# The sum of squares over channels: from a matmul with ones to a turn on VectorE and a DRAM scratch

## The chip, the cores and the metric

The kernel runs on one core of a Trainium2 chip. The time is device time in microseconds (us) from the first to the last instruction of one execution, the median over several. The kernel before takes 1737.63 us, median of 3 runs (1737.61 to 1738.3).

A core has TensorE (PE, matmuls and their weight loads), VectorE (DVE), ScalarE (ACT), GpSimd (POOL) and SyncE (SP), which here only issues DMAs. Each runs its own list of instructions in order; they wait for each other through semaphores. So an instruction that waits holds up all that stands behind it on its engine.

## The reference

Two sequences of 512 tokens with 512 channels go through a Mamba-2 block (128 heads in 8 groups) and a feed-forward block, each on the layer-normalised input with a residual. The part that matters here is the gated RMS norm of the Mamba block, per token and group of 1024 channels:

```
g = y * silu(gate)
gg = g.reshape(b, l, G, GS)                       # G = 8, GS = 1024
var = mean(gg * gg, axis=-1, keepdims=True)
g = (gg * rsqrt(var + EPS)).reshape(b, l, INTER) * norm_w
return g @ out_w.T
```

The kernel multiplies by `out_w` first and scales each token of the product by its `rsqrt` afterwards, when it adds it to the residual. So one number per token and group is wanted, `mean_sq`, with the tokens on the 128 partitions. `g` itself lies the other way round, channels on partitions and tokens along them, so the squares have to be summed across partitions.

## The kernel before, in words

All products are in float32 split in two parts (`_h` and `_l`), three matmuls each (`split_product`). Work goes in 64 steps, `K = 8 g + k`: 8 groups `g`, and in each `k` = 0 to 7, of which 0 to 3 are the four chunks of 128 tokens of the first sequence and 4 to 7 those of the second. The prediction calls `k` = 0 the first step of a group, `k` = 1, 2, 5, 6 second and third steps and `k` = 3, 7 fourth steps.

In a step TensorE does, in the order of `body`: the scores (`inside`, 32 matmuls, L1788), the total of the squares of the step before (`square_total`), the new state (`new_state`, not in fourth steps), a projection tile, turning x for the next step (`turn_x`), `match`, `across` (L1803), more projection tiles of the next sequence and group (L1712 to L1714, 12 matmuls each), and between them the two halves of the output product (`out_half`: L1846, L1829, L1836). Projection tiles go alternately into two PSUM banks, so tile i waits until tile i - 2 has been taken out: a gate tile by ScalarE, a convolution tile (`c0` to `c9`) by ScalarE and then three VectorE passes, the taps (L1385). The tiles of a slot are in `SLOT_TILES`: a first step has g0, g1, c0, c1, g2; a second c2, c3, c4, c5, g3; a third c6 to c9, g4; a fourth g5, g6, g7.

The squares: ScalarE squares g into `y` (8 blocks of channels by 128 tokens), GpSimd adds the 8 blocks to one (`square_sum`, `sum_ready`), TensorE multiplies that block by a column of ones (`square_total`, L1862), VectorE adds EPS (`mean_square`, L1481), GpSimd raises to -1/2 (`inverse_root`, L753), VectorE scales the output product and adds it up (`accumulate`, L1487).

Order is written out by hand on each engine. VectorE in a step: `fade`, `add_skip` (waits for the scores), `add_state`, `mean_square` of the step before, `gated`, and then taps, `scale_x` (L1404), `accumulate`, `scale_across`, the decay products (`scores`, L1415); in a first step also the low parts of the output weights (`ow_low`, L1391), which the output product needs. GpSimd in a fourth step: two masks (L710), a weight's low part (L704), `inverse_root`, two masks, `gT_low` (L738), `weigh_x` (L725), `square_sum`, `xw_low` (L733), which `new_state` of the next step waits for. SyncE: four decay loads of 256 KB, each when TensorE is through a quarter of the scores (`in_done`, L481), then ec loads (L487) and the weights of later tiles (L455).

Of the kernel before, what the change touches and what calls it, by code (L numbers as in the profile page):

```python
# [5 lines left out]
F32 = mybir.dt.float32  # L6
# [26 lines left out]
PIECE = KT * P  # L33

# [90 lines left out]
def build(nc, x_in, wp_in, ow_in, wdt_in, par_in, dt_bias_in, a_log_in,  # L125
# [3 lines left out]
    cols_dram = nc.dram_tensor("cols_scratch", (GROUPS, BATCH, P, UNIT_COLS), F32, kind="Internal").ap()  # L129
    cdec_dram = nc.dram_tensor("cdec_scratch", (BATCH, GROUPS, GH * SC), F32, kind="Internal").ap()  # L130

    with ExitStack() as ctx:
# [17 lines left out]
        sb("align", [P, 112])  # L150
# [110 lines left out]

        def total_of(K):

            return xt[1][:, 0:1] if K == MIDDLE else cbb[:, 2 * P:2 * P + 1]

# [65 lines left out]
        ss_done = sem("ss_done")  # L331
# [121 lines left out]
        def _(sp):  # L453
# [35 lines left out]

            def store_rows(b):  # L490
                cs = slice(b * SC, (b + 1) * SC)
                sp.dma_start(rows_dram[cs].rearrange("c h t -> h c t"),
                             ncumT[:, seq(b)].rearrange("p (c t) -> p c t", c=SC)).then_inc(rows_stored, 16)
# [102 lines left out]
            def last_chunk(k):  # L596
                K = LAST * CHUNKS + k
                if k < CHUNKS - 1:
                    for q in range(QUARTERS):
                        sp.wait_ge(in_done, K * QUARTERS + q + 1)  # L600
                        load_decay(LAST, k + 1, q)
                    sp.wait_ge(z_scaled, n_across(LAST, k + 1))
                    load_ec(LAST, k + 1)
                if k == SC:
                    load_up(WRING - 1)
                for p in LAST_PAIRS[k]:
                    if k == CHUNKS - 1 and p == LAST_PAIRS[k][-1]:
                        sp.wait_ge(g_ready, KEND)
                        sp.dma_start(b2_raw, l2_in[:, 0:HID]).then_inc(lora2_loaded, 16)
                        sp.dma_start(a2_raw, l2_in[:, HID:HID + FFN]).then_inc(lora2_loaded, 16)  # L610
                    load_up(2 * p + WRING)
                    load_up(2 * p + 1 + WRING)
                if k == CHUNKS - 1:
                    sp.wait_ge(in_done, KEND * QUARTERS)
                    for m in range(W2RING):
                        load_w2(m)

            def body(g, last):
                for k in range(CHUNKS):
# [21 lines left out]
                    if more:  # L641
                        for q in range(QUARTERS):
                            sp.wait_ge(in_done, K * QUARTERS + q + 1)
                            load_decay(gn, kn, q)
                    if more and kn % SC > 0:
                        if some(n_across(gn, kn)):
                            sp.wait_ge(z_scaled, n_across(gn, kn))
                        load_ec(gn, kn)
# [13 lines left out]
                    if last and k == SC - 1:  # L662
                        first_up()

# [226 lines left out]
        def _(act):  # L891
# [82 lines left out]
            def square(g, k):  # L974
                K, b, c = g * CHUNKS + k, k // SC, k % SC
                act.wait_ge(g_ready, K + 1)
                if some(K):
                    act.wait_ge(ss_done, K)
# [282 lines left out]
            act.wait_ge(ss_done, KEND)  # L1261
# [18 lines left out]
        def _(dve):  # L1280
# [283 lines left out]
            def last_chunk(k):  # L1564
                pairs = LAST_PAIRS[k]
                if k == SC:
# [12 lines left out]
                    return  # L1579
                gate_up(pairs[0] - 1)  # L1580
                fade(LAST, k)
                add_skip(LAST, k)
                add_state(LAST, k)
                mean_square(LAST, k - 1)
                gated(LAST, k)
# [7 lines left out]
                norm_apply(1, k - 1)  # L1593
                if k < CHUNKS - 1:
# [15 lines left out]
            def body(g, last):  # L1610
                for k in range(CHUNKS):
# [16 lines left out]
                    if late:  # L1628
                        norm_apply(1, 0)
                        norm_apply(1, 1)  # L1630
                    if k != 1:
                        fade(g, k)
# [5 lines left out]
                    else:  # L1638
                        add_state(g, k)
                        mean_square(*before)  # L1640
                        gated(g, k)
                    if late:
# [5 lines left out]
                        norm_apply(1, 2)  # L1648
                        for q in range(QUARTERS):
                            scores(gn, kn, q)  # L1650
# [58 lines left out]
        def _(pe):  # L1709
# [55 lines left out]
            def match(g, k):  # L1765
# [3 lines left out]
                if some(K - 1):  # L1769
                    pe.wait_ge(mean_ready, K - 1)  # L1770
# [37 lines left out]
            def new_state(g, k):  # L1808
# [8 lines left out]
                if K == MIDDLE + 1:  # L1817
                    pe.wait_ge(mean_ready, K)
# [141 lines left out]
            def last_chunk(k):  # L1960
                t = 2 * LAST_PAIRS[k][0]
                inside(LAST, k)
                if k > SC:
                    square_total(LAST, k - 1)
# [31 lines left out]
                else:  # L1996
# [7 lines left out]
                    square_total(LAST, k)  # L2004
# [4 lines left out]
            def body(g, last):  # L2009
                for k in range(CHUNKS):  # L2010
# [18 lines left out]
                    if not first:  # L2029
                        square_total(*((g, k - 1) if k else (g - 1, CHUNKS - 1)))  # L2030
# [15 lines left out]
                    if c == SC - 1:  # L2046
# [3 lines left out]
                        if last:  # L2050
                            norm_transpose(1, 2)
                            square_total(g, k)
# [21 lines left out]
            pe.wait_ge(mean_ready, KEND)  # L2074
# [111 lines left out]
```

## Time and profile before

| | |
|---|---|
| median of 3 runs | 1737.63 us |
| span of the profiled execution | 1737.2 us |
| TensorE, matmuls | 1724.5 us busy, 99% |
| TensorE, weight loads (beside matmuls) | 1436.9 us, 83% |
| VectorE | 1221.0 us, 70% |
| ScalarE | 1192.8 us, 69% |
| GpSimd | 1182.1 us, 68% |
| DMA queue of SyncE | 41.7% of 16 engines' span |
| mean granted TensorE clock | 0.999 |

Busy shares are means over the span. Within a step each engine has its own times of full work and of waiting. A timeline row gives the start in us from the span's start, the length, the engine and line, what is written and read, the number of instructions merged into the row, and in brackets the idle time before it. The length of merged rows is from the first start to the last end. The end of a matmul is modelled, and neighbours overlap, so differences between starts tell what a matmul costs.

### The profile page before, as it was taken

The page shows a single profiled execution, that of the slowest core. Times are in us where ns is not written, and L with a number is a line of the kernel's source. Part 1 is how long each engine was busy: PE and PEld are TensorE (multiplying, and loading weights), DVE is VectorE, ACT ScalarE, POOL GpSimd, SP SyncE. Part 2 cuts the span into 40 slices and gives each one's busy share as a digit, 9 for nine tenths or more (in the row PEclk, how much of TensorE's full clock was granted, in tenths as well). Part 3 has the DMA queues.
Part 4 walks back from the last instruction along what each step waited for, and adds up shares of the span by engine and source line. Part 5 has one row for each costly group of instructions (what it writes and reads, how often), then busy time and mean ns, then how long its engine had stood idle before and what let it go on. Part 6 is the DMA issues. An engine that isn't in the chain of part 4 may idle for free.

```text
span 1737.2 us, 27735 instructions
## 1 busy us (share of the span) xinstructions
PE 1724.5 (99%) x9925; PEld 1436.9 (83%) x9925; DVE 1221.0 (70%) x2154; ACT 1192.8 (69%) x2232; POOL 1182.1 (68%) x1058
## 2 busy tenths in 40 slices
PE   9999999999999999999999999999999999999999
PEld 7788888888888888888888888888888888787887
DVE  8886778768785769676875878586867688663323
ACT  6887677767867677767776777768777777663421
POOL 5586768677777668676867687766867686774510
PEclk9999999999999999999999999999999999999999
DMA  5534435343543443443534354345343353444201
GB/s 192 171 107 116 125 116 169 109 119 105 162 128 114 121 146 112 121 116 112 174 115 115 97 162 128 114 122 151 114 118 113 110 174 101 118 114 134 80 15 49
DMA packets 122056, 211.63 MB, mean 122 GB/s; under 512 B 24256, under 2 KB 28992, under 8 KB 121920
## 3 DMA queue, kind: packets, MB, share of 16 engines
q1 hardware_dynamic: 121920, 209.87, 41.7%
q8 instruction: 80, 1.31, 0.3%
q14 instruction: 56, 0.46, 0.1%
HBM read 205.09 MB, written 4.72 MB: 121 GB/s over the span
## 4 chain that ended last, share of the span: by engine, by line
PE 97%; DVE 1%; DMA 1%; POOL 0%; ACT 0%; issue 0%; POOLq 0%
PE bank L1712 19%; PE bank L1714 18%; PE bank L1713 18%; PE bank L1788 7%; PE bank L1846 7%; PE bank L1836 7%; PE bank L1829 7%; PE bank L1803 5%; PE bank L1762 2%; PE bank L2091 1%; PE bank L2092 1%; PE bank L2093 1%; PE bank L1862 1%; PE bank L1772 1%; PE bank L1953 1%; DMA w_raw<-in_wp 0%
## 5 line engine op out<-in xcount | busy, mean ns | idle before, releaser
L704 POOL TENSOR_TENSOR w_l<-w_raw,w_h 128x512 fp32r<-128x512 f32 x288 | 379.6, 1321 | 341.2 <-ACT w_h L900 341.2
L1712 PE MATMUL bank<-x_h,w_h 128*128 128x512 f32 (+1 forms) x1328 | 527.0, 397 | 3.9 <-DVE x_ch L1385 2.3
L1714 PE MATMUL bank<-x_h,w_l 128*128 128x512 f32 (+1 forms) x1328 | 519.7, 391 | 0.0
L1713 PE MATMUL bank<-x_l,w_h 128*128 128x512 f32 (+1 forms) x1328 | 518.1, 390 | 0.0
L1385 DVE SCALAR_TENSOR_TENSOR x_ch<-bank,par,x_ch 128x511 f32<-128x511 f32 (+2 forms) x384 | 287.2, 749 | 80.3 <-ACT x_ch L918 71.2
L953 ACT ACTIVATE decay<-decay,cols 128x128 f32<-128x128 f32 x1024 | 318.2, 390 | 3.7 <-DMA cdec<-cdec_scratch 1.6
L1712 PEld LDWEIGHTS bank<-x_h,w_h 128*128 128x128 f32 (+1 forms) x1328 | 249.5, 188 | 55.1 <-issue 3.1
L1714 PEld LDWEIGHTS bank<-x_h,w_l 128*128 128x128 f32 (+1 forms) x1328 | 249.2, 188 | 54.6
L1713 PEld LDWEIGHTS bank<-x_l,w_h 128*128 128x128 f32 (+1 forms) x1328 | 249.7, 188 | 51.1
L1415 DVE TENSOR_TENSOR decay<-decay,bank 128x512 f32<-128x512 f32 x256 | 171.3, 683 | 107.1 <-ACT decay L953 107.1
L918 ACT ACTIVATE x_ch<-bank,par 128x512 f32<-128x512 f32 x128 | 99.0, 774 | 185.6 <-PE bank L1714 185.5
L710 POOL TENSOR_SCALAR_AFFINE_SELECT decay<-decay 128x512 f32<-128x512 f32 x256 | 173.9, 697 | 65.8 <-DMA decay<-cum_scratch 64.3
L1436 DVE SCALAR_TENSOR_TENSOR bank<-x_ch,par,bank 128x128 f32<-128x128 f32 x512 | 138.4, 350 | 92.8 <-PE bank L1788 92.8
L900 ACT ACTIVATE w_h<-w_raw 128x512 fp32r<-128x512 f32 x288 | 178.7, 621 | 4.4 <-DMA w_raw<-in_wp 4.4
L738 POOL TENSOR_TENSOR gT_l<-sgT,gT_h 128x1024 fp32r<-128x1024 f32 x64 | 153.9, 2405 | 8.2 <-ACT gT_h L972 8.2
L939 ACT ACTIVATE sgT<-bank 128x512 f32<-128x512 f32 x122 | 71.9, 590 | 111.9 <-PE bank L1714 111.7
L1846 PE MATMUL bank<-ow_h,gT_h 128*128 128x512 f32 x512 | 137.3, 390 | 0.0
L1836 PE MATMUL bank<-ow_h,gT_l 128*128 128x512 f32 x512 | 136.9, 389 | 0.0
L1829 PE MATMUL bank<-ow_l,gT_h 128*128 128x512 f32 x512 | 136.9, 389 | 0.0
L1788 PEld LDWEIGHTS bank<-decay,xdt 128*64 128x64 f32 x2048 | 110.5, 137 | 22.6 <-issue 22.6
L1788 PE MATMUL bank<-decay,xdt 128*64 128x128 f32 x2048 | 125.9, 276 | 0.0
L733 POOL TENSOR_TENSOR xw_l<-xw,xw_h 128x1024 fp32r<-128x1024 f32 x48 | 114.9, 2394 | 0.3 <-ACT xw_h L965 0.3
(161 smaller groups left out, 2760.0 us busy)
## 6 DMA issues: line engine op xcount, KB each, us to landing
w_raw<-in_wp SPq DMA_DIRECT2D x288, 256.0 KB, 3.0
decay<-cum_scratch SPq DMA_DIRECT2D x256, 256.0 KB, 4.1
ec<-ecum_scratch SPq DMA_DIRECT2D x96, 256.0 KB, 6.2
ow_raw<-in_ow SPq DMA_DIRECT2D x64, 256.0 KB, 4.8
w_raw<-in_w SPq DMA_DIRECT2D x48, 256.0 KB, 2.7
acc<-in_x SPq DMA_DIRECT2D x8, 256.0 KB, 4.5
out<-acc SPq DMA_DIRECT2D x8, 256.0 KB, 2.0
cols<-cols_scratch SPq DMA_DIRECT2D x16, 96.0 KB, 2.7
```

The costliest lines, as they stand in the source:

```text
L704: pool.tensor_tensor(w_l[:, s, :], w_raw[:, s, :], w_h[:, s, :].bitcast(F32), ALU.subtract).then_inc(wl_ready, 1)
L710: pool.affine_select(out=d, in_=d, compare_op=ALU.is_ge, fill=fill, base=0, pattern=[[0, QH], [1, P]], channel_multiplier=-1).then_inc(mas ...
L900: act.activation(w_h[:, s, :], w_raw[:, s, :], ACT.Copy).then_inc(wh_ready, 1)
L953: last = act.activation(decay[:, h, :], decay[:, h, :], ACT.Exp, bias=cols[:, b, CUM, c, h:h + 1], scale=-1.0)
L1385: dve.scalar_tensor_tensor(out=conv(bu, t)[:, s:], in0=bank_of(u, i)[:, 0:SEQ - s], scalar=w, in1=conv(bu, t)[:, s:], op0=ALU.mult, op1=AL ...
L1712: pe.matmul(dst, wh, xh, start=(opens and k == 0), stop=False)
L1713: pe.matmul(dst, wh, xl, start=False, stop=False)
L1714: last = pe.matmul(dst, wl, xh, start=False, stop=(k == len(terms) - 1 and not more))
L1788: last = pe.matmul(yb[n // 4][a * HDIM:(a + 1) * HDIM, tok(n % 4)], xdt[:, h * HDIM:(h + 1) * HDIM], decay[:, h, :], start=(c == 0), stop= ...
L1829: last = pe.matmul(ob[:, :], gT_h[:, n, :], ow_l[:, n, :], start=False, stop=(k == 0 and n == CT - 1))
L1836: last = pe.matmul(ob[:, :], gT_l[:, n, :], ow_h[:, n, :], start=False, stop=(k > 0 and n == CT - 1))
L1846: pe.matmul(ob[:, :], gT_h[:, n, :], ow_h[:, n, :], start=(n == 0), stop=False)
```

## The change

`square_total` and its 64 matmuls go. In their place VectorE turns the summed block in squares of 32 by 32 (`turn_squares`) and adds up each 32 columns: partition 32 c + t then holds, in column b, the sum over the 32 channels of block c for token 32 b + t. SyncE stores that to a scratch in DRAM (`total_squares`), waits for the landing, and fetches it in four DMAs, one per 32 tokens, so that the four partial sums of a token come to lie side by side. VectorE adds those four and EPS. `mean_square` now stands behind `gated`. `match`, `new_state` and `accumulate`'s neighbours no longer wait for the old bank of the total. The line numbers of the changed kernel are 4 higher on SyncE, and 24 or more higher on VectorE.

```diff
+SQ = 32
+QUADS = P // SQ
...
+    sq_dram = nc.dram_tensor("sq_scratch", (2, P, QUADS), F32, kind="Internal").ap()
...
+            def total_squares(g, k):
+
+                K = g * CHUNKS + k
+                sp.wait_ge(sq_summed, K + 1)
+                sp.dma_start(sq_dram[K % 2], sq_part[:, :]).then_inc(sq_stored, 16)
+                sp.wait_ge(sq_stored, 16 * (K + 1))
+                if some(K):
+                    sp.wait_ge(mean_ready, K)
+                src = sq_dram[K % 2].rearrange("(c t) b -> b t c", c=QUADS)
+                for q in range(QUADS):
+                    sp.dma_start(sq_full[q * SQ:(q + 1) * SQ, :], src[q], allow_slow_non_contiguous=True).then_inc(sq_fetched, 16)
...
                         for q in range(QUARTERS):
                             sp.wait_ge(in_done, K * QUARTERS + q + 1)
                             load_decay(gn, kn, q)
+                            if q == 2 and some(K):
+                                total_squares(*((g, k - 1) if k else (g - 1, CHUNKS - 1)))
...
                     if last and k == SC - 1:
                         first_up()
+                        total_squares(g, k)
...
             def mean_square(g, k):
                 K = g * CHUNKS + k
-                dve.wait_ge(ss_done, K + 1)
-                dve.tensor_scalar(mean_sq[:, :], total_of(K), EPS, None, ALU.add).then_inc(mean_ready, 1)
+                dve.wait_ge(sq_fetched, 16 * QUADS * (K + 1))
+                dve.tensor_reduce(mean_sq[:, :], sq_full[:, :], mybir.AxisListType.X, ALU.add).then_inc(mean_step, 1)
+                dve.wait_ge(mean_step, K + 1)
+                dve.tensor_scalar(mean_sq[:, :], mean_sq[:, :], EPS, None, ALU.add).then_inc(mean_ready, 1)
+
+            def turn_squares(g, k):
+
+                K = g * CHUNKS + k
+                dve.wait_ge(sum_ready, K + 1)
+                dve.transpose(y[:, 1, :], y[:, 0, :]).then_inc(sq_turned, 1)
+                dve.wait_ge(sq_turned, K + 1)
+                if some(K):
+                    dve.wait_ge(sq_stored, 16 * K)
+                dve.tensor_reduce(sq_part[:, :], y[:, 1, :].rearrange("p (b t) -> p b t", b=QUADS),
+                                  mybir.AxisListType.X, ALU.add).then_inc(sq_summed, 1)
...
+                    if not first:
+                        turn_squares(*before)
                     if k != 1:
                         fade(g, k)
                     add_skip(g, k)
...
                         add_state(g, k)
+                        gated(g, k)
                         mean_square(*before)
-                        gated(g, k)
...
-                if some(K - 1):
-                    pe.wait_ge(mean_ready, K - 1)
...
-            def square_total(g, k):
-
-                K = g * CHUNKS + k
-                pe.wait_ge(sum_ready, K + 1)
-                if K == MIDDLE:
-                    pe.wait_ge(xdt_ready, K + 2)
-                pe.matmul(total_of(K), y[:, 0, :], ones[:, :], start=True, stop=True).then_inc(ss_done, 1)
...
-                    if not first:
-                        square_total(*((g, k - 1) if k else (g - 1, CHUNKS - 1)))
```

SyncE's list in the first step of a group, from the last output weight ahead of the decay loads on; `sq_part` and `sq_full` are the two small SBUF tiles, 128 by 4. Before:

```order
L469 DMA ow_raw<-in_ow 128x512
L481 DMA decay<-cum_scratch 128x512 [waits in_done] x4
L487 DMA ec<-ecum_scratch 64x1024 [waits z_scaled]
L487 DMA ec<-ecum_scratch 64x1024
L455 DMA w_raw<-in_wp 128x512 [waits pj_done]
```

and now:

```order
L473 DMA ow_raw<-in_ow 128x512
L485 DMA decay<-cum_scratch 128x512 [waits in_done] x3
L498 DMA sq_scratch<-sq_part 128x4 [waits sq_summed]
L504 DMA sq_full<-sq_scratch 32x4x1 [waits mean_ready,sq_stored]
L504 DMA sq_full<-sq_scratch 32x4x1 x3
L485 DMA decay<-cum_scratch 128x512 [waits in_done]
L491 DMA ec<-ecum_scratch 64x1024 [waits z_scaled]
L491 DMA ec<-ecum_scratch 64x1024
```

The fourth decay load, and all behind it, now stand behind a store, a wait for its landing and four fetches.

VectorE's list in such a first step, from `add_state` on; `ow_l` are the output weights' low parts. Before:

```order
L1475 COPY state<-bank 128x512 [waits st_done]
L1475 COPY state<-bank 128x512
L1481 TENSOR_SCALAR mean_sq<-bank 128x1 [waits ss_done]
L1449 TENSOR_TENSOR sgT<-bank,sgT 128x4x128 [waits y_ready,gate_done]
L1449 TENSOR_TENSOR sgT<-bank,sgT 128x4x128
L1391 SCALAR_TENSOR_TENSOR ow_l<-ow_raw,par,ow_h 128x512 [waits owh_ready] x2
L1404 TENSOR_TENSOR xdt<-bank,cols 128x512 [waits xw_ready,in_done,tx_done]
L1404 TENSOR_TENSOR xdt<-bank,cols 128x512
L1487 SCALAR_TENSOR_TENSOR acc<-bank,rstd,acc 128x512 [waits rstd_ready,out_done]
L1391 SCALAR_TENSOR_TENSOR ow_l<-ow_raw,par,ow_h 128x512 [waits owh_ready] x4
```

and now:

```order
L1499 COPY state<-bank 128x512 [waits st_done]
L1499 COPY state<-bank 128x512
L1473 TENSOR_TENSOR sgT<-bank,sgT 128x4x128 [waits y_ready,gate_done]
L1473 TENSOR_TENSOR sgT<-bank,sgT 128x4x128
L1505 TENSOR_REDUCE mean_sq<-sq_full 128x1 [waits sq_fetched]
L1507 TENSOR_SCALAR mean_sq<-mean_sq 128x1 [waits mean_step]
L1415 SCALAR_TENSOR_TENSOR ow_l<-ow_raw,par,ow_h 128x512 [waits owh_ready] x2
L1428 TENSOR_TENSOR xdt<-bank,cols 128x512 [waits xw_ready,in_done,tx_done]
L1428 TENSOR_TENSOR xdt<-bank,cols 128x512
L1524 SCALAR_TENSOR_TENSOR acc<-bank,rstd,acc 128x512 [waits rstd_ready,out_done]
L1415 SCALAR_TENSOR_TENSOR ow_l<-ow_raw,par,ow_h 128x512 [waits owh_ready] x4
```

The mean has moved behind `gated` (L1473) and waits for the fetches instead of the matmul; all the `ow_l`, `xdt` and `acc` work stands behind it.

## Rows read from the trace of the kernel before

**Rows 1.** The page, chain that ended last: share of the span by engine.

```profile
PE 97%; DVE 1%; DMA 1%; POOL 0%; ACT 0%; issue 0%; POOLq 0%
```

**Rows 2.** Groups of TensorE by line: busy us, mean ns of one, idle before.

```profile
L1862 PE MATMUL bank<-ones,y 128*128 128x1 f32 x128 | 24.4, 260 | 0.3 <-POOL y L748 0.3
```

**Rows 3.** Timeline (start us, length us), TensorE, step without a total.

```profile
82.67 1.97 PE L1788 MATMUL bank<-decay,xdt 128*64 128x128 f32 x32
...
84.90 0.40 PE L1713 MATMUL bank<-x_l,w_h 128*128 128x512 f32 x1
```

**Rows 4.** Timeline, TensorE: a fourth step and the next one.

```profile
717.12 1.97 PE L1788 MATMUL bank<-decay,xdt 128*64 128x128 f32 x32
...
734.14 1.97 PE L1788 MATMUL bank<-decay,xdt 128*64 128x128 f32 x32
...
736.28 0.48 PE L1712 MATMUL bank<-xw_h,b_tok_h 128*128 128x512 f32 x1
736.59 0.40 PE L1713 MATMUL bank<-xw_l,b_tok_h 128*128 128x512 f32 x1
```

**Rows 5.** Timeline, SyncE's queue, in the fourth step at 717.12.

```profile
717.81 1.75 SPq L481 DMA_DIRECT2D decay<-cum_scratch  x4
```

**Rows 6.** Its third decay load alone, issued at 718.7.

```profile
DMA to landing us min/median/max: 4.3/4.3/4.3
```

**Rows 7.** DMA issues: count, KB each, us from issue to landing.

```profile
out<-acc SPq DMA_DIRECT2D x8, 256.0 KB, 2.0
...
a_log<-in_a_log SPq DMA_DIRECT2D x1, 0.5 KB, 4.2
```

**Rows 8.** The second store of cdecT (2 KB), landing alone.

```profile
DMA to landing us min/median/max: 1.7/1.7/1.7
```

**Rows 9.** Groups of VectorE by line.

```profile
L1412 DVE TENSOR_TENSOR b_tok_l<-bank,b_tok_h 128x128 fp32r<-128x128 f32 x64 | 18.0, 281 | 0.0
...
L1481 DVE TENSOR_SCALAR mean_sq<-bank 128x1 f32<-128x1 f32 x64 | 9.7, 151 | 1.2 <-PE bank L1862 1.2
```

**Rows 10.** Timeline, GpSimd, fourth step at 717.12.

```profile
724.77 0.55 POOL L753 TENSOR_TENSOR rstd<-mean_sq,minus_half 128x1 f32<-128x1 f32 x1
...
733.31 2.38 POOL L733 TENSOR_TENSOR xw_l<-xw,xw_h 128x1024 fp32r<-128x1024 f32 x1
```

**Rows 11.** Timeline, TensorE, first step of a group.

```profile
640.30 1.97 PE L1788 MATMUL bank<-decay,xdt 128*64 128x128 f32 x32
...
656.74 1.07 PE L1829 MATMUL bank<-ow_l,gT_h 128*128 128x512 f32 x4
...
660.37 0.39 PE L1712 MATMUL bank<-x_h,w_h 128*128 128x512 f32 x1
```

**Rows 12.** Timeline, SyncE's queue, the same step.

```profile
642.78 2.17 SPq L481 DMA_DIRECT2D decay<-cum_scratch  x4
```

**Rows 13.** Its third decay load alone, issued at 643.7.

```profile
DMA to landing us min/median/max: 6.2/6.2/6.2
```

**Rows 14.** Timeline, VectorE, the same step.

```profile
646.58 1.41 DVE L1391 SCALAR_TENSOR_TENSOR ow_l<-ow_raw,par,ow_h 128x512 fp32r<-128x512 f32 x2
...
649.94 0.75 DVE L1487 SCALAR_TENSOR_TENSOR acc<-bank,rstd,acc 128x512 f32<-128x512 f32 x1 [0.76 <-POOL rstd L753]
650.61 5.26 DVE L1391 SCALAR_TENSOR_TENSOR ow_l<-ow_raw,par,ow_h 128x512 fp32r<-128x512 f32 x4
...
657.37 2.31 DVE L1385 SCALAR_TENSOR_TENSOR bcT<-bank,par,bcT 128x511 f32<-128x511 f32 x3
```

**Rows 15.** Timeline, TensorE, a second step.

```profile
759.74 1.97 PE L1788 MATMUL bank<-decay,xdt 128*64 128x128 f32 x32
...
771.66 0.39 PE L1712 MATMUL bank<-x_h,w_h 128*128 128x512 f32 x1
```

**Rows 16.** Timeline, VectorE, the same second step.

```profile
767.12 2.32 DVE L1385 SCALAR_TENSOR_TENSOR x_ch<-bank,par,x_ch 128x511 f32<-128x511 f32 x3 [1.01 <-ACT x_ch L918]
```

More of the change, by code:

```diff
@@ L149, in build @@
         mean_sq, rstd = sb("mean_sq", [P, 1]), sb("rstd", [P, 1])
-        sb("align", [P, 112])
+        sq_part, sq_full = sb("sq_part", [P, QUADS]), sb("sq_full", [P, QUADS])
+        sb("align", [P, 104])
         scan_ctx = ExitStack()
@@ L260, in build @@
         MIDDLE = (GROUPS - 1) * CHUNKS + SC - 1
-        def total_of(K):
-            return xt[1][:, 0:1] if K == MIDDLE else cbb[:, 2 * P:2 * P + 1]
         def normed(k, c, squares, gates):
@@ L330, in build @@
         out_done = sem("out_done")
-        ss_done = sem("ss_done")
+        sq_turned = sem("sq_turned")
+        sq_summed = sem("sq_summed")
+        sq_stored = sem("sq_stored")
+        sq_fetched = sem("sq_fetched")
+        mean_step = sem("mean_step")
         decay_seen = sem("decay_seen")
@@ L597, in last_chunk @@
                 K = LAST * CHUNKS + k
+                if k == CHUNKS - 1:
+                    total_squares(LAST, k - 1)
                 if k < CHUNKS - 1:
@@ L601, in last_chunk @@
                         load_decay(LAST, k + 1, q)
+                        if q == 2 and k > SC:
+                            total_squares(LAST, k - 1)
                     sp.wait_ge(z_scaled, n_across(LAST, k + 1))
@@ L614, in last_chunk @@
                     sp.wait_ge(in_done, KEND * QUARTERS)
+                    total_squares(LAST, k)
                     for m in range(W2RING):
@@ L977, in square @@
                 if some(K):
-                    act.wait_ge(ss_done, K)
+                    act.wait_ge(sq_summed, K)
                 act.activation(y[:, :, :], sgT[:, b, :, tok(c)], ACT.Square, scale=GCH ** -0.5).then_inc(sq_ready, 1)
@@ L1260, in _ @@
             act.wait_ge(out_done, 2 * KEND)
-            act.wait_ge(ss_done, KEND)
+            act.wait_ge(sq_summed, KEND)
             for m in range(FT):
@@ L1579, in last_chunk @@
                     return
+                turn_squares(LAST, k - 1)
                 gate_up(pairs[0] - 1)
@@ L1583, in last_chunk @@
                 add_state(LAST, k)
+                gated(LAST, k)
                 mean_square(LAST, k - 1)
-                gated(LAST, k)
                 if k < CHUNKS - 1:
@@ L1593, in last_chunk @@
                 norm_apply(1, k - 1)
+                if k == CHUNKS - 1:
+                    turn_squares(LAST, k)
                 if k < CHUNKS - 1:
@@ L1648, in body @@
                         norm_apply(1, 2)
+                        turn_squares(g, k)
                         for q in range(QUARTERS):
@@ L1816, in new_state @@
                     pe.wait_ge(x_l_ready, CHUNKS + k - 1)
-                if K == MIDDLE + 1:
-                    pe.wait_ge(mean_ready, K)
                 for h in range(2):
@@ L1962, in last_chunk @@
                 inside(LAST, k)
-                if k > SC:
-                    square_total(LAST, k - 1)
                 new_state(LAST, k)
@@ L2003, in last_chunk @@
                     out_half(LAST, k, 1)
-                    square_total(LAST, k)
                     up(t + 4)
@@ L2051, in body @@
                             norm_transpose(1, 2)
-                            square_total(g, k)
                         out_half(g, k, 1)
@@ L2073, in _ @@
             pe.wait_ge(lora2_l_ready, 2)
-            pe.wait_ge(mean_ready, KEND)
             pe.wait_ge(acc_ready, KEND)
```

## The prediction

> **What bounds the kernel now.** I read the page first, then the groups by line, then timelines of three kinds of step. The chain that ended last is TensorE for 97% of the span [rows 1], so the time is TensorE's own work plus whatever makes it wait; nothing off TensorE shortens it. The removed total is in 128 matmul records (two for each of 64 totals), 24.4 us busy in sum, with 0.3 us of waiting in the whole run [rows 2]. Work beside TensorE is free until it makes one of TensorE's waits come true, so what matters is how much room each wait has. I call a step's start T, the moment its first L1788 matmul starts; there are 64 steps, eight to a group.
>
> **What is removed.** Matmuls overlap, so 24.4 us is not what goes. In step 0, which has no total, the second product behind the scores starts 84.90 - 82.67 = 2.23 us after T [rows 3]; with a total in between it is 736.59 - 734.14 = 2.45 us [rows 4]. So one total costs 0.22 us, 64 of them 14.1 us. The upper end is 24.4 us, the lower 0. The wait of `match` for `mean_ready` also goes; it ended no idle time of TensorE worth a row, so nothing is late in its place and I take 0.
>
> **What is added, and on which path.** The mean square of a step is now made in the next one: VectorE turns and sums (`turn_squares`), SyncE stores 2 KB, waits for the landing, issues four fetches, and VectorE finishes in `mean_square`, behind which its own queue stands still. SyncE does this between the third and the fourth decay load.
>
> *When the mean is there, ordinary step.* The four decay loads start at 717.81 and take 1.75 us to issue, 0.44 each [rows 5], so the third is out at T + 2.0 and the store goes at T + 2.0. That third load lands 4.3 us after its issue at 718.7, at T + 5.9 [rows 6]. The store has the same queue and the same DMA engines as the three loads of 256 KB ahead of it. Bounds for its landing: 1.7 us after issue, as a 2 KB store did with little else in flight [rows 8], which is T + 3.7, and 4.2 us, as a 0.5 KB load did behind other transfers [rows 7], T + 6.2. I take T + 6.0, just behind the load ahead, since that is the nearest row in the same place. Four fetches at 0.44 us start from T + 6.1, the last at T + 7.4. Each has 128 pieces of 4 bytes; its landing lies between 1.7 [rows 8] and 4.2 us [rows 7]. I take 2.0, the row of the stores at the end, which also go through an empty queue [rows 7]: T + 9.4. The reduction and the addition are 0.15 us each by the tiny operation they replace [rows 9], 0.1 for the semaphore between them: the mean is ready at T + 9.8. SyncE itself comes 5.8 us later (T + 7.8 instead of 2.0) to the fourth decay load, the ec loads and the next weights. Behind them GpSimd's fourth mask and ScalarE's w_h wait; by the timelines the mask has its turn just behind the later rstd anyway and the weights are needed four tiles ahead, so I count 0 there and keep up to 1 us per step for the range.
>
> The Trainium skill weighs in twice here, from "DMA: Bandwidth & Descriptors". Its section "Anatomy of one DMA" gives a DMA a fixed 2.0 us and very little for size: the store would then land at T + 4.0 whatever is ahead of it, which is the first rival below. Its section "Queues, rings and completion order" says that an engine takes a queue's descriptors in ring order and that the completion write lands only behind earlier writes: that gives T + 6.0, my value. No run so far shows a 2 KB store behind decay loads.
>
> *Fourth steps* (positions 3 and 7 of groups 0 to 6: 14). GpSimd starts rstd at 724.77 and then runs without a gap through masks, gT_l, xw, the square sum and xw_l, which ends at 735.69: 10.92 us [rows 10]. TensorE needs xw_l at 736.28, 0.59 us later [rows 4]. After: rstd starts at T + 9.85, xw_l ends at T + 20.8. TensorE gets there at 17.02 + 1.90 = T + 18.9 (next T, then 32 score matmuls and no total). It waits 1.9 us, in all 14 x 1.9 = 26 us.
>
> *First step of a group* (7, groups 1 to 7). SyncE starts its decay loads only at 642.78 [rows 12], behind parameter, weight and ow loads. The third lands 6.2 us after 643.7, at T + 9.6 [rows 13]. The same sum gives store landed 9.7, last fetch issued 11.1, down at 13.1, mean at T + 13.5. VectorE stood at T + 6.3 before where its ow_l starts [rows 14] and its queue is nearly full: two ow_l (1.41) to 14.9, xdt (1.2) to 16.2, acc (0.7) to 16.9, four ow_l (5.26, so 2.6 for two) to 19.5 and 22.1, state fade (1.5) to 23.6, the taps of tile c0 (2.3) to 25.9 [rows 14]. TensorE wants the fourth ow_l at 656.74, T + 16.4, and c0's bank for tile g2 at 660.37, T + 20.1 [rows 11]; both come 0.2 earlier without the total. It waits 19.5 - 16.2 = 3.3, and then 25.9 - (19.9 + 3.3) = 2.7 us: 6.0 a group, 42 us.
>
> *Second and third steps* (positions 1, 2, 5, 6; 30 in all, 23 without those right behind a first step). VectorE's taps of the slot's first tile stand behind `mean_square`: they start at 767.12 now and take 2.32 [rows 16]; after, T + 9.8 + 2.3 = 12.1. TensorE writes over that bank at 771.66, T + 11.9 [rows 15], 11.7 without the total: 0.4 us, 23 x 0.4 = 10 us.
>
> *The rest.* `turn_squares` is two operations over 128 columns, 0.3 us each by the row of that size [rows 9], before add_skip, where VectorE idles for PE in most steps; it costs where VectorE is late, in the step behind a first one. With step 3 of group 7, where the store stands behind the first FFN weights, I put 8 us for all this, 3 to 15 for the range. Moving `gated` ahead of the mean is what keeps g_half in time; it gains 0.1 us at most.
>
> Sum: 26 + 42 + 10 + 8 = 86 us of waits, less 14 us. The profiled execution spans 1737.2 us and the median of the runs is 1737.6, 0.4 more. So 1737.6 + 72, about 1809 us.
>
> **Rivals.**
> *Short landings.* The store lands 2.0 us after its issue, not behind the loads. Ordinary steps have the mean at T + 7.8, xw_l ends at 18.8 against 18.9: no wait. In a first step the third load is issued at T + 3.9, so the store is down at 5.9, the mean at 9.7: taps end at 22.1 against 19.9, 2.2 us, 7 x 2.2 = 15. With 4 for the rest: 1737.6 + 19 - 14 = 1743 us. For it: landings of 1.7 and 2.0 us exist [rows 7, 8]; against: both have nothing big ahead.
> *Slow small pieces.* Each fetch takes the 4.2 us of the 4-byte-piece load [rows 7], so the mean is 2.2 us later: fourth steps 4.1 x 14 = 57, first steps 8.2 x 7 = 57, second and third 2.6 x 23 = 60, rest 10; 184 - 14 gives 1908 us. For it: the only row with such pieces. Against: that load stood behind others of 256 KB at the start.
> *All hidden, faster.* Only the 0.22 us per total counts: 1737.6 - 14 = 1723.5 us. The point that decides is the mean in a first step: the taps there end 12.4 us behind it, so at T + 7.5 or sooner TensorE waits for nothing. But even the third decay load lands at T + 9.6 there. It would need the store to overtake and VectorE to have slack that its timeline doesn't show.
>
> **How the numbers follow.** Forecast 0.65, short landings 0.16, slow pieces 0.14, hidden 0.05. Within the forecast, a landing 0.5 us sooner or later moves the mean by as much in 44 steps, 22 us, and the rest by 7: 1780 to 1840. For 8 in 10 I reach towards both rivals: 1752 to 1880. A change within 0.2% (3.5 us) can't be told from none here. Hidden is faster; of short landings a fifth or so may come out same or faster. Faster 0.06, same 0.03, slower 0.91.
>
> **What would show it.** Right: TensorE has new waits, for xw_l in the step behind a fourth one (about 1.9 us), for ow_l and for x_ch or bcT taps in a first step (3.3 and 2.7); VectorE's idle time before the reduction of sq_full is 3 to 5 us in ordinary steps and about 7 in first ones, ended by the DMA; the store of sq_part lands about 4 us after issue in ordinary steps, 5.5 in first ones; fetches land 2 us after issue. Wrong: if the store lands in 2 us (short landings), if the fetches need 4 (slow pieces), if masks wait for the fourth decay load and so add a price that I put at 0, or if TensorE waits in all steps alike.

## The result, and the profile after

The changed kernel takes 1856.24 us, median of 4 runs (1853.38 to 1859.18), against 1737.97 us (1737.61 to 1738.37) for the kernel before beside it: 118 us more, ratio 1.0677, 95% interval 1.0662 to 1.0692. The profiled execution spans 1855.5 us at a mean granted clock of 0.988. The forecast was 1809, its range 1752 to 1880: the sign and part of the mechanism held, and the forecast was 47 us short.

The page after: busy time by engine, and the chain that ended last, by engine and by line (answers to [rows 1]).

```profile
PE 1767.1 (95%) x9797; PEld 1432.5 (77%) x9797; DVE 1246.6 (67%) x2346; ACT 1195.8 (64%) x2232; POOL 1188.3 (64%) x1058
...
PE 62%; DMA 17%; DVE 10%; SPq 5%; issue 3%; POOL 3%; ACT 1%; POOLq 0%; DVEq 0%
PE bank L1755 11%; PE bank L1757 11%; PE bank L1756 11%; DMA sq_scratch<-sq_part 9%; PE bank L1829 6%; PE bank L1875 6%; PE bank L1885 5%; PE bank L1868 5%; DMA decay<-cum_scratch 3%; SPq L504 3%; DMA sq_full<-sq_scratch 3%; DVE ow_l L1415 2%; PE bank L1844 2%; DVE x_ch L1409 2%; POOL gT_l L762 2%
```

TensorE was 97% of the chain and is 62%. The landing of the small store alone is 9% of the span, more than 150 us of the chain for 64 stores of 2 KB. TensorE is idle for 1855.5 - 1767.1 = 88.4 us, before 1737.2 - 1724.5 = 12.7: 75.7 us of new waits. Who ends them stands in the list of TensorE's waits after (total us, times, longest). "issue" means that the profile shows no releaser; the x_ch wait of 2.4 us stands in the kernel before too, with 2.3:

```profile
PE bank L1875 <- POOL gT_l L762: 22.9, 14, 2.1
PE bank L1755 <- DVE x_ch L1409: 14.2, 18, 2.4
PE bank L1755 <- DVE bcT L1409: 13.8, 7, 2.0
PE bank L1755 <- issue: 10.3, 11, 1.0
PE bank L1885 <- issue: 5.3, 7, 1.2
PE bank L1755 <- POOL xw_l L757: 3.5, 1, 3.5
```

The largest, for `gT_l`, is none that the prediction had. The groups of three of the new instructions on VectorE, and of two on ScalarE and GpSimd that wait longer for DMAs than before, where it was 4.4 us for w_h and 65.8 for decay (busy us, mean ns of one, idle before and its releaser):

```profile
L1505 DVE TENSOR_REDUCE mean_sq<-sq_full 128x1 f32<-128x4 f32 x64 | 10.1, 157 | 224.0 <-DMA sq_full<-sq_scratch 224.0
L1513 DVE STREAM_TRANSPOSE y<-y 128x128 f32<-128x128 f32 x64 | 19.5, 304 | 5.6 <-POOL y L772 5.6
L1517 DVE TENSOR_REDUCE sq_part<-y 128x4 f32<-128x128 f32 x64 | 18.3, 286 | 2.2
...
L924 ACT ACTIVATE w_h<-w_raw 128x512 fp32r<-128x512 f32 x288 | 179.3, 623 | 87.5 <-DMA w_raw<-in_wp 87.5
L734 POOL TENSOR_SCALAR_AFFINE_SELECT decay<-decay 128x512 f32<-128x512 f32 x256 | 175.3, 698 | 92.4 <-DMA decay<-cum_scratch 91.6
```

VectorE stands idle for 224 us, 3.5 a step, in front of the mean. Issues to landing (count, KB each, median us), which answer to [rows 7, 8]:

```profile
sq_full<-sq_scratch SPq DMA_DIRECT2D x256, 0.5 KB, 1.8
...
sq_scratch<-sq_part SPq DMA_DIRECT2D x64, 2.0 KB, 3.6
```

*A fourth step and the head of the next.* The timelines after, first of SyncE's queue, then of GpSimd, then of TensorE; T, the start of the first score matmul, is 860.28. They answer to [rows 4, 5, 10].

```profile
860.98 1.28 SPq L485 DMA_DIRECT2D decay<-cum_scratch  x3
862.30 0.43 SPq L498 DMA_DIRECT2D sq_scratch<-sq_part  x1
865.84 1.74 SPq L504 DMA_DIRECT2D sq_full<-sq_scratch  x4
867.62 0.43 SPq L485 DMA_DIRECT2D decay<-cum_scratch  x1
```

```profile
869.41 0.56 POOL L777 TENSOR_TENSOR rstd<-mean_sq,minus_half 128x1 f32<-128x1 f32 x1 [1.64 <-DVE mean_sq L1507]
869.93 0.65 POOL L734 TENSOR_SCALAR_AFFINE_SELECT decay<-decay 128x512 f32<-128x512 f32 x1
872.07 0.64 POOL L734 TENSOR_SCALAR_AFFINE_SELECT decay<-decay 128x512 f32<-128x512 f32 x1 [1.50 <-DMA decay<-cum_scratch]
872.67 2.37 POOL L762 TENSOR_TENSOR gT_l<-sgT,gT_h 128x1024 fp32r<-128x1024 f32 x1
...
879.46 2.37 POOL L757 TENSOR_TENSOR xw_l<-xw,xw_h 128x1024 fp32r<-128x1024 f32 x1
```

```profile
872.60 1.07 PE L1868 MATMUL bank<-ow_l,gT_h 128*128 128x512 f32 x4
875.09 1.19 PE L1875 MATMUL bank<-ow_h,gT_l 128*128 128x512 f32 x4 [1.42 <-POOL gT_l L762]
876.12 1.08 PE L1885 MATMUL bank<-ow_h,gT_h 128*128 128x512 f32 x4
877.04 1.07 PE L1868 MATMUL bank<-ow_l,gT_h 128*128 128x512 f32 x4
...
881.93 0.47 PE L1755 MATMUL bank<-xw_h,b_tok_h 128*128 128x512 f32 x1 [1.02 <-issue]
```

The reader is to see one thing after another: the store goes at T + 2.0 and is down at T + 5.5, the fetches go, and only then, at T + 7.3 instead of T + 2.0, the fourth decay load. It lands at T + 11.6. GpSimd has done rstd and the third mask by T + 10.3, stands 1.50 us for that load, and `gT_l`, next on its list, is 1.42 us late for TensorE. `xw_l` ends at 881.83 and TensorE starts 0.1 later, another 1.02 us lost. The profile names no releaser for that wait, but in all ten such rows TensorE starts 0.1 us behind the end of `xw_l`.

*The first step of a group.* The chain that ended last, in order of time (start, length, what), in the step at 878.94; it answers to [rows 11 to 14].

```profile
882.38 5.45 DMA sq_scratch<-sq_part
887.84 0.32 SPq L504
...
890.41 1.78 DMA sq_full<-sq_scratch
...
892.22 0.17 DVE mean_sq L1505
...
892.48 1.21 DVE ow_l L1415 x2
...
895.09 0.66 DVE acc L1524
895.75 4.05 DVE ow_l L1415 x4
899.80 1.57 DVE state L1482
901.37 0.67 DVE bcT L1409
...
903.74 0.47 PE bank L1755
```

It is the chain that the prediction wrote down for the second wait of such a step, link by link: store, fetch, mean, ow_l, acc, ow_l, state, taps, and TensorE waiting for the bank.

### The profile page after: what moved, and what is told of

Same layout as the page of the kernel before. It is cut to its first block, busy times and chain, and to the rows that moved or that the text cites. A ratio compares the mean times of both kernels' runs of the same rounds, so it can differ in the third digit from the quotient of the medians.

```text
span 1855.5 us, 28055 instructions
## 1 busy us (share of the span) xinstructions
PE 1767.1 (95%) x9797; PEld 1432.5 (77%) x9797; DVE 1246.6 (67%) x2346; ACT 1195.8 (64%) x2232; POOL 1188.3 (64%) x1058
## 4 chain that ended last, share of the span: by engine, by line
PE 62%; DMA 17%; DVE 10%; SPq 5%; issue 3%; POOL 3%; ACT 1%; POOLq 0%; DVEq 0%
PE bank L1755 11%; PE bank L1757 11%; PE bank L1756 11%; DMA sq_scratch<-sq_part 9%; PE bank L1829 6%; PE bank L1875 6%; PE bank L1885 5%; PE bank L1868 5%; DMA decay<-cum_scratch 3%; SPq L504 3%; DMA sq_full<-sq_scratch 3%; DVE ow_l L1415 2%; PE bank L1844 2%; DVE x_ch L1409 2%; POOL gT_l L762 2%
## 5 line engine op out<-in xcount | busy, mean ns | idle before, releaser
L1755 PE MATMUL bank<-x_h,w_h 128*128 128x512 f32 (+1 forms) x1328 | 539.4, 406 | 30.6 <-DVE x_ch L1409 14.2
L1757 PE MATMUL bank<-x_h,w_l 128*128 128x512 f32 (+1 forms) x1328 | 528.9, 398 | 0.0
L1756 PE MATMUL bank<-x_l,w_h 128*128 128x512 f32 (+1 forms) x1328 | 528.8, 398 | 0.0
L1409 DVE SCALAR_TENSOR_TENSOR x_ch<-bank,par,x_ch 128x511 f32<-128x511 f32 (+2 forms) x384 | 286.6, 747 | 10.8 <-ACT x_ch L942 1.6
L924 ACT ACTIVATE w_h<-w_raw 128x512 fp32r<-128x512 f32 x288 | 179.3, 623 | 87.5 <-DMA w_raw<-in_wp 87.5
L1875 PE MATMUL bank<-ow_h,gT_l 128*128 128x512 f32 x512 | 140.5, 397 | 22.9 <-POOL gT_l L762 22.9
L1505 DVE TENSOR_REDUCE mean_sq<-sq_full 128x1 f32<-128x4 f32 x64 | 10.1, 157 | 224.0 <-DMA sq_full<-sq_scratch 224.0
L1885 PE MATMUL bank<-ow_h,gT_h 128*128 128x512 f32 x512 | 144.0, 404 | 8.1 <-issue 5.3
L1460 DVE SCALAR_TENSOR_TENSOR bank<-x_ch,par,bank 128x128 f32<-128x128 f32 x512 | 138.1, 349 | 18.4 <-PE bank L1829 18.2
L1868 PE MATMUL bank<-ow_l,gT_h 128*128 128x512 f32 x512 | 141.6, 399 | 0.0
L1875 PEld LDWEIGHTS bank<-ow_h,gT_l 128*128 128x128 f32 x512 | 96.3, 190 | 48.9 <-POOL gT_l L762 29.0
```

The source lines that it names most:

```text
L924: act.activation(w_h[:, s, :], w_raw[:, s, :], ACT.Copy).then_inc(wh_ready, 1)
L1409: dve.scalar_tensor_tensor(out=conv(bu, t)[:, s:], in0=bank_of(u, i)[:, 0:SEQ - s], scalar=w, in1=conv(bu, t)[:, s:], op0=ALU.mult, op1=AL ...
L1755: pe.matmul(dst, wh, xh, start=(opens and k == 0), stop=False)
L1756: pe.matmul(dst, wh, xl, start=False, stop=False)
L1757: last = pe.matmul(dst, wl, xh, start=False, stop=(k == len(terms) - 1 and not more))
L1868: last = pe.matmul(ob[:, :], gT_h[:, n, :], ow_l[:, n, :], start=False, stop=(k == 0 and n == CT - 1))
```

## The experiments

Two theories stood at first. **A**: VectorE and all behind it wait for the mean. **B**: SyncE's queue, standing still for the store, brings the fourth decay load and later loads late, whoever needs the mean. A third, **C**, came later, from a number that neither explained.

**The DMAs kept, but nobody waits for the fetches.** (This kernel and the two without DMAs leave out the sum across partitions.)

```diff
-                dve.wait_ge(sq_fetched, 16 * QUADS * (K + 1))
-                dve.tensor_reduce(mean_sq[:, :], sq_full[:, :], ...
+                dve.wait_ge(sq_summed, K + 1)
+                dve.tensor_reduce(mean_sq[:, :], sq_part[:, :], ...
```

> Store, wait and fetches of the changed kernel stay on SyncE, but VectorE's mean reads the partial sums of its own partition and waits for no fetch (the sum over partitions is left out). Theory A, that the late mean in VectorE's queue costs most: the 118 us fall to about 20 (1745 us), and fourth steps are back near 17 us. Theory B, that SyncE's blocked queue costs most (the fourth decay load goes out at T + 7.3 instead of 2.0, so GpSimd's fourth mask and gT_l behind it come late): fourth steps stay at 18.7 us or more, and only the first steps get short; 1770 us or more.

1811.61 us, ratio 1.0413 [1.0397, 1.0428]. Only 45 of the 118 us hang on the wait for the mean. TensorE still waits 28.9 us for `gT_l`, 15 times, and fourth steps still take 18.4 to 23.0 us, against 17.0 before. First steps fall back to 26 to 27 us from 29 to 32: there it is the mean. So A alone is refuted, and over half of the loss must lie elsewhere.

**No DMAs at all.** As the last one, and `total_squares` returns at once.

> As the changed kernel, with the turn and sums on VectorE, but no store and no fetch; the mean reads the partial sums of its own partition (the sum over partitions is left out). Both theories: all waits go, and what is left is 0.22 us less per total: 1737.6 - 14 = 1724 us, at most 3 more for the turn. If the turn itself is dear, 1730 or more.

1747.69 us, ratio 1.0050 [1.0031, 1.0069]. So SyncE's waits and the traffic cost 1811.6 - 1747.7 = 64 us. TensorE was idle for 59.9 us in the last kernel and is for 13.2 in this one; 38 us of the difference are its waits for `gT_l` and `xw_l`, as B says. But 1724 was expected, and this has no new waits of TensorE worth a row. With the total gone its steps should be 0.22 us shorter. Most take 25.75 us instead of 25.61, and fourth steps 16.95 instead of 17.02. Something of the change costs over 20 us and is neither A nor B.

**Where SyncE stops: behind the fourth decay load, or ahead of all four.**

```diff
-                            if q == 2 and some(K):
+                            if q == 3 and some(K):
```

> The changed kernel with store, wait and fetches behind the fourth decay load instead of ahead of it. Theory A: the mean comes 0.5 to 1 us later, so 10 to 25 us slower than the changed kernel (1866 to 1880). Theory B: the fourth mask is no longer late, so fourth steps lose about 1 us each and the whole is faster, 1835 to 1845. Both at once: near 1856.

1863.57 us, ratio 1.0711 [1.0695, 1.0727]. Fourth steps fall (17.7 to 18.5 us in most groups) and no wait for `gT_l` is left in the list. But VectorE's wait for the mean grows from 224.0 to 270.6 us, 0.7 a step, and TensorE waits 28.5 us for the x_ch taps where it waited 14.2. What one place gains the other gives back. The time lies between the two ranges, 2 us below A's, and fourth steps moved as B says.

> The changed kernel with store, wait and fetches ahead of all four decay loads. The store has nothing big ahead of it in ordinary steps and should land in 1.7 to 2 us, the mean is ready at about T + 6, and all decay loads go out 3.3 us later. Theory A: about 1770. Theory B: the masks of fourth steps come 1 to 3 us late, 1790 or more.

With `total_squares` ahead of the four loads: 1819.03 us, ratio 1.0458 [1.0440, 1.0475]. First steps take 27.2 to 28.1 us instead of 29 to 32, while `gT_l` still costs 8.7 us in 18 waits. That lies in B's range (1790 or more), but the shorter first steps are A's: both theories carry part of the time. The store of this kernel, with no load ahead of it in its own step, lands 1.4 us after its issue (median); behind three loads it took 3.6:

```profile
sq_scratch<-sq_part SPq DMA_DIRECT2D x64, 2.0 KB, 1.4
```

**The total twice, in the kernel before**, to measure its price.

> The kernel before, with each total's matmul made twice. If a total costs TensorE 0.22 us, as the starts behind it say, 64 more cost 14 us: 1752. If it costs its share of the chain (0.31 us), 20 us: 1758. If it hides, nothing.

1751.54 us against 1737.95, ratio 1.0072 [1.0058, 1.0086]: 13.6 / 64 = 0.21 us each. The gain of the change was sized right.

**Turn, store and fetches early**, in the step that makes the squares, so that nothing waits for a landing.

```diff
-                            if q == 2 and some(K):
-                                total_squares(*((g, k - 1) if k else (g - 1, CHUNKS - 1)))
...
-                        total_squares(g, k)
+                    total_squares(g, k)
...
-                    if not first:
-                        turn_squares(*before)
...
+                    if c < SC - 1:
+                        turn_squares(g, k)
                     taps_of(tiles[3:-1])
...
+                    if c == SC - 1:
+                        turn_squares(g, k)
```

> The changed kernel with the turn put in the step of the squares itself (behind the third decay product, in fourth steps at the end) and store, wait and fetches at the end of SyncE's list of that step, behind its last weight load. In three of four steps the mean has then landed about when the next step starts, in fourth steps at T + 6 of the next, and decay loads are late only there, by 3 us. Theory A and B both: 1724 to 1732, faster than both kernels. If the fetches at a step's start collide with something else, 1740 or more.

1780.27 us, ratio 1.0238 [1.0223, 1.0253]. The forecast missed by 50 us, although second steps of the second half of a group (k = 5) have no wait. Again the steps without a wait are longer than they should be, 25.7 us where 25.4 were due.

```diff
-        sb("align", [P, 104])
+        sb("align", [P, 96])
```

> The kernel before, with nothing of the change, whose filler is 8 elements longer, so every tensor behind it starts 32 bytes further, as in the changed kernel. Placement theory: 24 us slower than before, 1762 us, steps of 25.9 us, the projection's three matmuls 0.70 us. Rival: 1738 us, unchanged.

> The kernel without the DMAs (VectorE takes the mean from its own partial sums, so the sum over partitions is left out), as before, with one thing changed: the filler tensor is 8 elements shorter, so every tensor behind it starts at the byte it has in the kernel before instead of 32 bytes further. Placement theory: the projection's three matmuls are back at 0.68 us from 0.70, 1328 such triples at 6 ns a matmul give 24 us, so 1724 us and steps of 25.4 us. Rival (the slower matmuls come from the order of the instructions, the turn's traffic or the missing total): 1747 us, unchanged.

> The changed kernel with the filler 8 elements shorter, every later tensor at its old address. Placement theory: 24 us less than 1856, so 1832 us, within 8 us of it, with the waits of TensorE unchanged in sum (76 us). Rival: 1856, unchanged; or more than 10 us above 1832 if a faster projection only leaves TensorE waiting longer for the same transfers.

> The kernel with turn, store and fetches in the step of the squares (1780 us), with the filler shorter as well. Placement theory: 24 us less, 1756 us; still above the kernel before by about 18 us, which its own waits make. Rival: 1780, unchanged.

| kernel | shifted by 32 bytes | at the old bytes | difference |
|---|---|---|---|
| before | 1760.08 (ratio 1.0131 [1.0116, 1.0147]) | 1737.58 | 22.5 |
| change without DMAs | 1747.69 | 1729.20 (0.9948 [0.9935, 0.9960]) | 18.5 |
| change | 1856.24 | 1841.10 (1.0593 [1.0579, 1.0608]) | 15.1 |
| early | 1780.27 | 1761.65 (1.0141 [1.0127, 1.0155]) | 18.6 |

C is shown, in both directions and without anything else of the change. A gain of 24 us was forecast for each of the three kernels put back to the old bytes, and they gained 15 to 19: TensorE's busy time fell by 18 to 23 us, but its idle time grew by 2.0, 5.3 and 3.2 us. Without the DMAs and at the old bytes the steps are back at 25.37 and 16.78 us, 0.24 shorter than before the change, as the missing total wants it. TensorE's groups by line, of the kernel before and of the same kernel shifted (mean ns behind the comma):

```profile
L1712 PE MATMUL bank<-x_h,w_h 128*128 128x512 f32 x1312 | 520.6, 397 | 3.9 <-DVE x_ch L1385 2.3 <-POOL w_l L704 1.5
L1714 PE MATMUL bank<-x_h,w_l 128*128 128x512 f32 x1312 | 513.4, 391 | 0.0
...
L1846 PE MATMUL bank<-ow_h,gT_h 128*128 128x512 f32 x512 | 137.3, 390 | 0.0
L1836 PE MATMUL bank<-ow_h,gT_l 128*128 128x512 f32 x512 | 136.9, 389 | 0.0
```

```profile
L1712 PE MATMUL bank<-x_h,w_h 128*128 128x512 f32 x1312 | 526.1, 401 | 3.1 <-DVE x_ch L1385 2.2 <-POOL w_l L704 0.9
L1714 PE MATMUL bank<-x_h,w_l 128*128 128x512 f32 x1312 | 518.7, 395 | 0.0
...
L1846 PE MATMUL bank<-ow_h,gT_h 128*128 128x512 f32 x512 | 139.0, 393 | 0.0
...
L1836 PE MATMUL bank<-ow_h,gT_l 128*128 128x512 f32 x512 | 136.9, 389 | 0.0
```

Each of 3936 projection matmuls is 4 to 5 ns slower, 11 us in these two groups and 6.6 more in the third, L1713: 17.4 of the 21.7 us by which TensorE is busier. Of their operands only the weights are shifted. In the output product both operands are shifted, and there L1836 is not slower at all and L1846 1.7 us in sum. Why the one product suffers and the other hardly does was not told apart, nor were shifts other than 32 bytes tried. In the early kernel the other 32 us above 1729 are new waits for 22.5 us (37.7 us of idle TensorE against 15.2), small ones by many releasers, the largest `bcT` taps with 5.1 us in 9 waits. VectorE now turns and adds in front of them; that this is the cause no run shows.

**B by itself**: the changed kernel at the old bytes, with the store where it was and SyncE's wait and the four fetches behind the fourth decay load.

```diff
                             if q == 2 and some(K):
                                 total_squares(...)
+                            if q == 3 and some(K):
+                                fetch_squares(...)
```

> The changed kernel at its old addresses (1841 us), with SyncE's wait for the store and the four fetches moved behind the fourth decay load; the store keeps its place behind the third. Queue theory (what costs the fourth steps is that SyncE waits with the fourth decay load behind the store, so that GpSimd's last mask and gT_l come late): the fourth load is issued near T+3 instead of T+7.5, the 25 us that TensorE waits for gT_l go, fourth steps fall from a mean of 19.6 us to 18.3, 14 of them and the step behind each give 25 to 30 us: 1811 to 1816 us. Rival (the fetches now stand behind the fourth load's packets and land later, which all steps pay): the mean comes near T+11 and the time stays at 1841 us or above.

1822.32 us, ratio 1.0477 [1.0463, 1.0492], 19 us less than 1841. SyncE's queue and GpSimd in one of its fourth steps, T = 750.6:

```profile
752.66 0.43 SPq L498 DMA_DIRECT2D sq_scratch<-sq_part  x1
753.13 0.43 SPq L485 DMA_DIRECT2D decay<-cum_scratch  x1
756.18 1.74 SPq L507 DMA_DIRECT2D sq_full<-sq_scratch  x4
```

```profile
760.24 1.23 POOL L744 TENSOR_SCALAR_AFFINE_SELECT decay<-decay 128x512 f32<-128x512 f32 x2
761.43 2.42 POOL L772 TENSOR_TENSOR gT_l<-sgT,gT_h 128x1024 fp32r<-128x1024 f32 x1
```

The fourth load goes at T + 2.5, the masks run without a gap, `gT_l` starts 10.8 us after T instead of 12.4, and of TensorE's 25.4 us for it 0.2 are left. Fourth steps fall from 19.7 to 17.9 us, below the 18.3 expected. In this step the mean is not later (T + 9.0). Over the run it is somewhat: VectorE waits 243.1 us for it instead of 213.6, and TensorE's waits for the x_ch taps grew from 13.8 to 21.5 us and those for `xw_l` from 10.4 to 14.6. So the time stayed 6 to 11 us above the forecast. B's mechanism is shown. The rival is refuted as to the time and the size of the delay, but its mechanism costs a little.

**A kernel that beats both**: before, with a cheaper total.

```diff
-                pool.tensor_tensor(y[:, 0, :], y[:, 0, :], y[:, 1, :], ALU.add)...
+                pool.tensor_tensor(y_r[:, 0, :], y[:, 0, :], y[:, 1, :], ALU.add)...
...
-                pe.matmul(total_of(K), y[:, 0, :], ones[:, :], start=True, stop=True)...
+                pe.matmul(total_of(K), y_r[:, 0, :], ones_r[:, :], start=True, stop=True)...
```

> The kernel before, all of it, with the total as a single-pass matmul: GpSimd's last addition writes the rounded type, and the ones are of that type (two columns of them, at the old addresses of everything else). No part of the change is in it. If the 0.22 us of a total are mostly its four passes in full fp32, some 0.15 us of each go: 64 x 0.15 = 10 us, so 1728 us, a kernel faster than both. Rival: the 0.22 us are the load of the 128 x 128 block, which stays: 1738 us.

1729.12 us against 1739.53, ratio 0.9945 [0.9933, 0.9958]. Its total in TensorE's groups:

```profile
L1864 PE MATMUL bank<-ones_r,y_r 128*128 128x2 f32 x64 | 17.2, 269 | 0.0
```

There is one record for each total instead of two [rows 2]. The time saved is 10.4 us, and 10.4 / 64 = 0.16 us of the 0.22 of a total. This kernel is as fast as the kernel that has no total and no DMAs at all (1729.20): three quarters of what the change was after can be had on TensorE, with nothing new to wait for.

## Why the prediction was right or wrong

*Removed: right.* 0.22 us a total, measured 0.21 by doubling it.

*When the mean is there: right.* The store in an ordinary step was put down just behind the third load, at T + 6.0; in the ordinary steps of groups 3 and 4 it is there at 5.3 to 6.7, in most 0.2 to 0.3 us behind that load. Put ahead of the loads it landed in 1.4 us, and behind four of them in 3.9 (medians of the two kernels that move the stop), so it is the loads ahead that make it late. Fetches were given 2.0 us and take 1.8. The mean was due at T + 9.8 and is ready at 869.33, T + 9.1; in the first step 13.5 was forecast and 892.56 - 878.94 = 13.6 came. That refutes both landing rivals. One slip in the short one: it has the third load of a first step issued at T + 3.9, which is when the store goes; the load goes at T + 3.4. Of the two rules of the Trainium skill, "DMA: Bandwidth & Descriptors", the one in "Queues, rings and completion order" agrees with the trace (3.6 us median for 2 KB, behind the load ahead of it). The fixed 2.0 us of "Anatomy of one DMA", which that section gives for DMAs issued by GpSimd, are near what SyncE's fetches take in a queue that has run empty (1.8 us). For the store they don't hold, with 1.4 us ahead of the loads and 3.6 behind them, and the measurement decides.

*Fourth steps: the step that failed.* "Behind them GpSimd's fourth mask and ScalarE's w_h wait; by the timelines the mask has its turn just behind the later rstd anyway ... so I count 0 there." For `w_h` that holds: ScalarE waits 87.5 us for the weights, and TensorE only 1.5 for `w_l`. For the mask it fails. The fourth load, issued 5.3 us later, lands at T + 11.6, when GpSimd is through with rstd and the third mask, and the price falls on `gT_l`, which the sum had at no risk. The prediction kept up to 1 us a step for this in its range and named it among the signs of being wrong. Measured are 1.4 us for `gT_l` and 1.0 for `xw_l` behind it, 2.4 us where 1.9 was forecast for `xw_l` alone; in sum 22.9 + 10.3 = 33 us instead of 26. Taking that load out from behind the store gave 19 us back, and then the path that the prediction had, rstd to `xw_l`, cost 1.0 us a step (14.6 us in 15 waits) and not 1.9. So it is partly luck that 33 lies near 26. The sum has a slip as well: the next step's start at T + 17.02 still has a total in it, and without it the forecast wait is 2.1 us.

*First steps: the path is right, one wait is another, and the size is half.* 6.0 us a group were forecast, 42 in all. In the group shown 1.10 + 1.98 = 3.1 are recorded, and 5.3 + 13.8 = 19 in all seven. The second wait, for the taps, is as forecast (1.98 us for 2.7). The first, 3.3 us for the fourth ow_l, isn't there. In all seven groups TensorE goes on 0.10 us after acc ends (895.75 here), so it waits there for the output bank, 0.2 to 1.2 us; no profile row names the releaser. Four ow_l take 4.13 us in VectorE's list here, against 5.26 in [rows 14], so all behind them is 1.1 us earlier. And the sum counts a wait twice: a first step stands behind a fourth one, so by the forecast TensorE is already 1.9 us late there for `xw_l`, which leaves 1.4 of the 3.3 us. By the prediction's own rows 13 us of the 42 are too much.

*Second and third steps: right in kind and in sum.* 10 us were forecast. Of the 14.2 us of x_ch waits 2.3 stood there before, so 12 are new. They are not 0.4 us in each of 23 steps but 17 waits of 0.15 to 1.18 us, some of them in the step behind a first one, which the 23 left out.

*The sum of the waits: 86 forecast, 75.7 recorded.* That is near, but by errors that cancel: 7 us more in fourth steps, 23 less in first ones, 2 more in second and third, and 3.5 more for the rest. *What the time has beyond that is what I put at nothing:*

| | us |
|---|---|
| 64 totals gone | -14 |
| new idle time of TensorE | +76 |
| placement, 15 to 22 by four pairs | +18 |
| half clock: 44.4 us of the span at the lower clock (mean 0.988), 4.5 before, half of the difference lost (an estimate) | +20 |
| left over | +18 |

Part of what is left over is visible: a wait costs more than its idle record. In the rows of the fourth step the starts of L1868 and L1875 are 2.49 apart where 0.92 is usual, 1.57 lost, and those of the next pair 1.03, another 0.11: 1.68 for a record of 1.42. With 0.2 for each of some 60 waits that would be 12 us; this is an estimate, and 6 stay open. Nor can the half clock be separated by an experiment here; its share is worked out. The four executions of the changed kernel fit it in kind: 1859.18 us at a mean clock of 0.987, 1853.38 at 0.992.

A different view of the same 118 us, by kernels that differ in one thing: 45 for VectorE's wait for the mean, 64 for SyncE's wait and the traffic, 18.5 for placement, and -8.4 for what remains (total gone, turn and sums added).

## What to carry to other kernels

A wait put into a DMA-issuing queue delays everything behind it in that queue: follow each of the delayed loads to its consumer and then one instruction further, and issue what is independent before waiting. When a change adds or removes small tiles, compare the start bytes of all the others, and keep them, before reading the time. To shorten an operation on the bound engine, first try to make it cheaper where it is; here that gave 10 us, and moving it through DRAM cost 118, 15 to 22 of them by placement.

## What the runs showed of the hardware that was not expected

Tiles shifted by 32 bytes cost 22.5 us of 1737.6 with no instruction changed, 17.4 of them in the matmuls of x_h or x_l with the weights. In the kernel before the tiles behind the filler start at multiples of 64 bytes, in the shifted one 32 bytes off; whether 64 is the number that matters no run shows.

Behind many of TensorE's new waits stands a stretch at its lower clock. In the windows of the changed kernel (window, length, busy time with count, granted clock, DMA share, GB/s), around the wait of 1.98 us that ended at 903.74:

```profile
900.00:904.00 4.00, 2.02 (x9) 1.00 0.25 66
904.60:908.00 3.40, 3.40 (x10) 0.50 0.00 0
908.00:911.00 3.00, 3.00 (x14) 1.00 0.00 0
```

At 0.50, 1.2 instead of 2.4 GHz, ten matmul records fill 3.4 us with no idle time between them and no DMA running, and projection matmuls start 0.43 us apart instead of 0.23. The kernel before spends 4.5 us of its span at that clock, the changed one 44.4, in twelve stretches. Each of the twelve begins inside a wait of TensorE or at most 1.3 us behind its end, and these waits are 1.77 to 3.32 us long. But five other waits of 1.90 to 3.47 us are followed by none. Of the two kernels without DMAs, which have no new waits, one spends nothing of its span there and the other 7.4 us. So it seems that waits of the bound engine are in part paid twice; this is read from the times, and no experiment separates it.
